# Strip passes of a graph network kernel: each gather of a far group waits for two more expanded pairs

## What is computed

```python
# second layer, for each of its three weight matrices (norm is taken apart into node factors)
h = x @ Ws[i]
x = relu(segment_sum(norm[:, None] * h[src], dst, num_segments=n) + bs[i])
# last layer
agg = segment_sum(x[src], dst, num_segments=n)
```

## Time and profile before

| what | value |
|---|---|
| median of 3 runs | 21405.54 us (21394.11 to 21519.8) |
| the profiled execution: span | 21435.5 us |
| TensorE matmul busy | 13504.4 us (63%) |
| TensorE weight load busy | 11403.1 us (53%) |
| VectorE busy | 9802.8 us (46%) |
| ScalarE busy | 5857.0 us (27%) |
| GpSimd busy | 9834.1 us (46%) |
| mean granted TensorE clock | 0.762 |
| the four strip passes, from their first matmul to their last | 1194.5, 1202.5, 1202.4, 1205.4 us |

### The profile page before, as it was taken

One profiled execution on the slowest core, in us unless ns is written; L12 is line 12 of the kernel. 1 busy time (PEld: TensorE's weight loads), 2 busy tenths in 40 slices (PEclk: granted clock), 3 DMA queues, 4 the chain that ended last, 5 costly groups with the idle time before them and its releaser, 6 DMA issues. The chain is left out here.

```text
span 21435.5 us, 385420 instructions
## 1 busy us (share of the span) xinstructions
PE 13504.4 (63%) x124067; PEld 11403.1 (53%) x124067; DVE 9802.8 (46%) x18585; ACT 5857.0 (27%) x11169; POOL 9834.1 (46%) x10022
## 2 busy tenths in 40 slices
PE   0344444557556656666777677767777776777465
PEld 0222223556446655565666566656656665666465
DVE  8444545446861211212555555555555455554313
ACT  0000000112553333333333333333333333333233
POOL 0455554662754344343444444444444444444342
PEclk9555565555678877777888788888988897888677
DMA  2211111111654344343333233323323332333343
GB/s 80 43 40 39 39 40 39 52 52 49 212 190 117 107 117 115 109 116 102 82 82 85 60 83 83 81 64 85 87 62 83 81 87 61 82 85 79 86 115 89
DMA packets 1281223, 1800.52 MB, mean 84 GB/s; under 512 B 558054, under 2 KB 817510, under 8 KB 1279974
## 3 DMA queue, kind: packets, MB, share of 16 engines
q1 hardware_dynamic: 978113, 1423.30, 22.5%
q0 software_dynamic: 296960, 327.11, 7.8%
q10 hardware_dynamic: 5040, 35.13, 0.4%
HBM read 1475.83 MB, written 308.76 MB: 83 GB/s over the span
## 5 line engine op out<-in xcount | busy, mean ns | idle before, releaser
L1163 POOL DMA_INDIRECT rows_buf<-feature_table,idx_buf x4320 | 4408.7, 1021 | 4727.7 <-DMA idx_buf<-src_idx 3116.0
L886 POOL DMA_INDIRECT rows_buf<-feature_parts,idx_buf x2176 | 2058.5, 946 | 2854.2 <-PE banks L941 1890.4
L928 PE MATMUL banks<-sums_space,tmp 128*128 128x192 bf16 x13720 | 2110.7, 279 | 1581.0 <-issue 1074.8
L898 ACT ACTIVATE sums_space<-banks 128x384 bf16<-128x384 f32 x3920 | 1642.3, 454 | 3278.1 <-PE banks L915 2357.4
L1243 PE MATMUL banks<-table_parts,tmp 128*128 128x64 bf16 x36750 | 1652.4, 202 | 1383.4 <-issue 1248.0
L928 PEld LDWEIGHTS banks<-sums_space,tmp 128*128 128x128 fp8e4 x13720 | 1473.3, 138 | 1827.6 <-issue 1805.9
L915 PE MATMUL banks<-table_parts,tmp 128*128 128x192 bf16 x13720 | 2087.1, 276 | 297.8 <-DMA tmp<-one_hots 280.0
L1243 PEld LDWEIGHTS banks<-table_parts,tmp 128*128 128x128 fp8e4 x36750 | 1421.6, 104 | 1588.7 <-issue 1582.5
L735 POOL DMA_INDIRECT rows_buf<-attention_table,idx_buf x1664 | 1575.0, 947 | 1438.0 <-DVE parts L1465 884.0
L1219 PE MATMUL banks<-attr_buf,params 128*128 128x256 f32 x5660 | 1907.9, 458 | 355.0 <-issue 180.5
L1314 DVE TENSOR_TENSOR onehot<-banks,early 128x448 f32<-128x448 f32 x875 | 545.5, 623 | 3349.2 <-remote 1308.5
(11 more groups left out here) (395 smaller groups left out, 21625.1 us busy)
## 6 DMA issues: line engine op xcount, KB each, us to landing
tmp<-one_hots SPq DMA_DIRECT2D x1855, 448.0 KB
attr_buf<-cell_attr SPq DMA_DIRECT2D x875, 128.0 KB
one_hots<-tmp SPq DMA_DIRECT2D x245, 448.0 KB
attr_buf<-attr SPq DMA_DIRECT2D x653, 128.0 KB
rows_buf<-feature_table,idx_buf POOLq DMA_INDIRECT x4320
gathered_rows<-rows_buf SPq DMA_DIRECT2D x208, 272.0 KB
rows_buf<-gathered_rows SPq DMA_DIRECT2D x208, 272.0 KB
rows_buf<-feature_parts,idx_buf POOLq DMA_INDIRECT x2176
```

The costliest lines, as they stand in the source:

```text
L886: pool.indirect_dma_start(out=far_rows[:, u, t, :], out_offset=None, in_=table3, in_offset=bass.IndirectOffsetOnAxis(ap=idx_buf[:, u, t:t ...
L898: act.activation(cell_rows[:, q, 0:width], bank[q][:, 0:width], ACT.Copy).then_inc(s_cells_sb, 1)
L928: ins = pe.matmul(bank[4 + h][:, half * 3 * D:(half + 1) * 3 * D], dst_cells[:, k, :, j, half], cell_rows[:, q, j % 2 * 3 * D:(j % 2 + 1) ...
L1163: pool.indirect_dma_start(out=edge_rows[:, u, t, :], out_offset=None, in_=table, in_offset=bass.IndirectOffsetOnAxis(ap=idx_buf[:, u, t:t ...
```

## The change

GpSimd's part of the strip pass is written anew; no other engine's part is touched. The groups, buffers, gathers and their order stay. The first gather of a group waits as before. Each of the other seven also waits until TensorE has finished a further number of expansions: for the first group of a strip 13/8 of an expansion per gather (counts 13, 15, 16, 18, 20, 21 and 23 of the strip), for the second 15/8 (26, 28, 30, 32, 34, 36 and 38; those above 28 are reached in the next strip). The first four groups of a pass stand outside the loop: the first is gathered without such a wait, the other three with one expansion for each gather. With each wait goes a `sem_inc` of `s_turn`.

```diff
             @block.gpsimd
             def _(pool):
-                with pool.Fori(0, FARG // U) as i:
-                    for u in range(U):
-                        pool.wait_ge(s_idx[u], (i + 1) * 16)
-                        pool.wait_ge(s_sum, i * U + (u + 1))
-                        pool.sem_inc(s_turn, 1)
-                        for t in range(G):
-                            pool.indirect_dma_start(
-                                out=far_rows[:, u, t, :], out_offset=None, in_=table3,
-                                in_offset=bass.IndirectOffsetOnAxis(ap=idx_buf[:, u, t:t + 1], axis=0),
-                            ).then_inc(s_rows[u], 16)
+                def gather_tile(u, t):
+                    pool.indirect_dma_start(
+                        out=far_rows[:, u, t, :], out_offset=None, in_=table3,
+                        in_offset=bass.IndirectOffsetOnAxis(ap=idx_buf[:, u, t:t + 1], axis=0),
+                    ).then_inc(s_rows[u], 16)
+
+                def first_group(g):
+                    pool.wait_ge(s_idx[g], 16)
+                    pool.sem_inc(s_turn, 1)
+                    for t in range(G):
+                        if g > 0:
+                            pool.wait_ge(s_cells, (3, 11, 19)[g - 1] + t)
+                            pool.sem_inc(s_turn, 1)
+                        gather_tile(g, t)
+
+                def group_behind(i, h, n):
+                    u, expansions = 2 * h + n, (12, 25)[n]
+                    pool.wait_ge(s_idx[u], (i + 2) * 16)
+                    pool.wait_ge(s_sum, i * U + (u + U + 1))
+                    pool.sem_inc(s_turn, 1)
+                    for t in range(G):
+                        if t > 0:
+                            pool.wait_ge(s_cells, i * (2 * CHUNKS * OPS) + (h * CHUNKS * OPS + expansions + (13, 15)[n] * t // G))
+                            pool.sem_inc(s_turn, 1)
+                        gather_tile(u, t)
+
+                for g in range(U):
+                    first_group(g)
+                with pool.Fori(0, (NS - 3) // 2) as i:
+                    for h in range(2):
+                        for n in range(2):
+                            group_behind(i, h, n)
```

## The result

| what | before | after |
|---|---|---|
| median of the runs on one chip, 4 each | 21399.83 us (21373.76 to 21519.8) | **20390.1 us** (20385.87 to 20393.68) |
| ratio after/before, 95% interval | | 0.9521 (0.9502 to 0.954) |
| profiled execution: span | 21435.5 us | 20386.0 us |
| mean granted TensorE clock | 0.762 | 0.783 |
| the four strip passes, first to last matmul | 1194.5, 1202.5, 1202.4, 1205.4 us | 943.4, 941.9, 941.2, 940.3 us |

The kernel is 4.8% faster, 1010 us by the medians; the prediction had 608 us. The four strip passes add up to 4804.8 us before and 3766.8 us after. These 1038 us are nearly the whole difference of the two spans (1049.5 us). The passes with edge features kept their times: from their first gather to their last some 1798 to 1833 us each, against 1807 to 1831.

What follows compares the result with a forecast made beforehand. Close gathers delaying TensorE's completion word were taken to bound the strip passes. Saving 4.9 us on each of 124 strips gave 608 us, other terms 0: 21405.5 - 608 = 20798 us, range 20100 to 21550.

Steps and rivals of the forecast that it cites:

- what the stall is and that it feeds back: Strip passes: close gathers delay word of TensorE's completions to ScalarE; with waits, missing counts stop GpSimd, ending the delay sooner.
- N cycles of 2.14 us overhead, so 20.0 + 2.14N: Strip time: 16 gathers in N cycles, each adding restart and release; N = 4.5 gives 29.6 us, against 34.5.
- hold: Strip passes: word of TensorE's completions reaches ScalarE late during close gathers, until 2.6 us after the last one's start.
- N = 3: Lower time bound, three cycles a strip: 26.4 us a strip, saving 1004 us, time 20401 us.
- N = 4 warm: Strip passes: seven expansions, so four gathers, a cycle, TensorE keeping its clock: 28.6 us a strip.
- N = 5.3 cold: Strip passes: every cycle begins with TensorE at the low clock and passes 5.3 expansions: 31.3 us a strip.
- a met wait costs 0: GpSimd's added waits: one already met costs 0, an unmet one 0.79 us behind the event.
- no copy with over 2.6 us of idle: Sign in the profile after: no ScalarE copy of the strip passes has over 2.6 us of idle before it.
- no row of five: Sign in the profile after: no five ScalarE copies follow one another together, as they did after a burst before.
- A: Rival, strip passes: delay vanishes, GpSimd's 20.0 us bounds a strip; saving 1798 us, time 19608 us; chance 0.12.
- B: Rival, strip passes: no gain, stall is a price per gather (1.1 us) or cycles number 6.5; 21405 us; chance 0.14.
- C: Rival, strip passes: slower, two gathers a cycle, 37.1 us a strip, 322 us more, 21728 us; chance 0.14.

Runs made afterwards that it cites:

- c1b: The changed kernel with all added waits kept but counts so low they are met at once, on a chip with a hold: 21578.9 us, ratio 1.0048 to before.
- c2_loop_only: The changed kernel without added waits in the first four groups of a pass, on a chip without a hold: 14999.45 us, ratio 1.0 to before.
- c1: The changed kernel with all added waits kept but met at once, on a chip without a hold: 14995.35 us, ratio 0.9998 to before.
- c3b: The changed kernel with only one wait a group, before its fifth gather, on a chip with a hold: 20490.93 us, ratio 0.9558 to before.
- c4b: The changed kernel with waits only before gathers 2, 4 and 6 of a group, on a chip with a hold: 20514.09 us, ratio 0.956 to before.
- first four experiments: Changed kernel with waits met at once, loop waits only, one wait a group, or three; all on a chip where before takes 14998.9 us: 14995.35 to 15003.9 us.
- c5: The changed kernel with each gather waiting for the landing of the previous one in its group, not for expansion counts: 24080.62 us, before 21464.37.
- c6: The kernel before with plain GpSimd transfers of the same 48 KB in place of the strip gathers, unpaced: 19081.14 us, before 21464.37.
- c7: The kernel before with gathered rows of 64 bytes instead of 384, same count and indices, unpaced: 21519.15 us, before 21464.37.

## Why the prediction was right, and where it was off

**Right: what the stall is and that it feeds back.** TensorE's work isn't slow; word of its completion is late while gathers follow closely, and is given out in a body when they pause. The trace of before shows the delay itself. This is the expansion of the pair whose copy starts at 6819.15, 8.5 us after these matmuls end:

```profile
6810.30 0.33 PE L915 MATMUL banks<-table_parts,tmp 128*128 128x192 bf16 x2
```

TensorE's increments of `s_cells` are recorded late too, at 6812.04, 6814.90 and then from 6819.13 on. One reading of the prediction was too strong: of the five copies from 6819.15, four had finished pairs waiting; TensorE ran the fifth pair after the release. So it is in after, where three pairs had been ready at 6619.53. That release comes 0.75 us before the next run of gathers. The runs of three to four came: by my count of all of after's gathers (a new run where two starts are over 1.45 us apart), 231 runs of three and 183 of four, with 111 single ones, 88 pairs and 35 of five, a mean of 3.2. The restarts are mostly released by TensorE's line, and from the first copy of the release to the gather it takes 0.75 us and 0.88 us, for a forecast 0.79 from the event. The clock is over 0.80, the other passes are unchanged. The gaps of 3 to 4 us between runs didn't come; the full stop shown has 2.74 us from start to start. c1b shows that it is the pacing and not the presence of the waits.

**Mis-sized: the term for a stop.** The step "N cycles of 2.14 us overhead, so 20.0 + 2.14N" had a form that holds, as the waits of after add up by it, with both numbers off. There are 5.5 stops and not 4.5, and one costs 1.2 us and not 2.14. The price failed because I took the release of 2.6 us from a burst of eight and used it for a run of four. There it is 1.93 to 1.99 us: a full stop costs 1.5 us (2.74 between starts less 1.25). And it failed because many stops aren't at the end of a hold at all: GpSimd only waits a little for a count, 1.46 us of idle on average (168.2/115) where the full stop shown has 1.80. Strip: 26.7 for 29.6 us, 2.9 x 124 = 360 us of the 402 us by which the saving was too small.

The two errors work against each other. With the right number of stops at the old price a strip would be 31.8 us and the saving 335 us; part of the nearness of the forecast is luck. And 20390 us lies just below the forecast's own lower bound (N = 3, 20401 us); only the allowance of the range below N = 3, down to 20100, takes it in.

**The clock.** The middle between N = 4 warm and N = 5.3 cold was taken because the traces of before did not say what short stalls do. They leave the clock high: 1.00 in the cycle shown, 0.93 over 680 us, where 0.80 stood before. The rule of the Trainium skill (TensorE: Matmul & The Clock Gate, "Loop structure matters more than you think") that the prediction weighed names long waits between matmuls as what brings the clock down. These rows are in line with it. At 28.6 us the forecast would still have been short by 1.9 us a strip, so the clock was the smaller part of the error.

**Missed: the first strips.** Strip 0 was counted at 0, plus or minus 15 us a pass. Timed to the end of its 28th copy, by my count it takes 63.0 to 65.2 us in before and 43.7 to 46.2 us in after, 77 us less over the four passes (the 57 us and the 14 us a pass in the expectation of c2_loop_only are not in the trace). Part of it comes back in strip 1, 36.8 to 39.9 us against 34.4 to 36.5. There the counts are already met, 16 gathers go out in one row from 6285.98 on, and a copy waits longer than in any burst of eight of before (at most 6.1 us):

```profile
6305.70 0.49 ACT L920 ACTIVATE sums_space<-banks 128x384 bf16<-128x384 f32 x1 [10.91 <-remote]
```

The mean of strips 1 to 31 is 27.1 us for 34.8, 948 us over 124 strips. With strip 0, and 12 us of strip 32 (22 us for 25.1), which had been counted as unchanged, these are the 1038 us that the passes lost. Whether the waits of the first four groups alone make strip 0 faster stays open, since c2_loop_only ran only where there is no hold.

**Missed: "a met wait costs 0", "no copy with over 2.6 us of idle" and "no row of five".** c1b shows the first as wrong where there is a hold, by 91 us in all (ratio 1.0048, 1.0023 to 1.0073), and right where there is none (c1: 0.9998). The row of five occurs in after too: three pairs stand ready at the release, and TensorE finishes the next two while they are copied. And 26 rows of ScalarE in the 680 us have more than 2.6 us of idle before them, up to the 3.90 us at 6597.71 shown above: a copy can wait through two close gathers and the release behind them, and the release alone was no bound for it.

**The rivals.** A (20.0 us a strip) did not come from the edit, but its figure was exactly what a chip without a hold gives: 20.0 us. B fell: after, c3b and c4b cut the stall in half with the same gathers (6.7 to 7.9 us a strip over 20.0, for 14.5). C fell: runs of two are few, and even c4b, whose waits allow them, went on mostly in fours (370 runs, against 136 pairs, by my count with a bound of 1.5 us) and gained.

## What to carry to other kernels

If copies or other work behind an engine come in a body after a burst of indirect gathers from GpSimd, don't look at the sum of the gathers' time but at how long they follow one another without a pause; cut the row by waiting for the progress of the engine that is held, once in the middle of a group first, since that is most of the gain. Don't wait for the gather's own landing: that costs more than the hold. Try the same in each pass that has such a row, and on more than one chip, for a stall may be absent from one.

## What the hardware showed that I had not expected

- Indirect gathers of GpSimd 1.25 us apart keep word of TensorE's completions from ScalarE. Word the other way isn't held. In the burst of the earlier trace rows a copy ends at 6815.42 (6814.93 + 0.49), and the aggregation that reads it starts 0.14 us later, by TensorE's timeline of before (0.14 to 0.15 us also behind the copies of 6812.06 and 6819.15):

```profile
6815.56 0.51 PE L928 MATMUL banks<-sums_space,tmp 128*128 128x192 bf16 x4 [2.02 <-issue]
```

  Gathers 3.2 to 3.3 us apart don't do it (c5), nor do plain transfers from the same queue 0.53 us apart (c6), and it doesn't depend on the bytes (c7). What in the chip does it stays open.
- Two chips: the same kernel takes 21.4 ms on one and 15.0 ms on another, with gathers just as close. The one without a hold was met once, in the first four experiments; wherever else the kernel before ran it took 21.4 to 21.5 ms. I know no cause.
- One gather of GpSimd costs 1.25 us of its queue, a plain transfer of the same size 0.53 us, and from the start of a gather to the next, with a wait for its landing between them, it takes mostly 3.2 to 3.3 us (c5).
- Waits that are met at once leave the gathers' spacing as it is, yet on a chip with a hold 472 more of them a pass made the kernel 0.5% longer (c1b).
- The end of the hold depends on the length of the run: it comes 1.75 us after the start of the last gather of three, 1.91 us of four, 2.65 us of eight.
